# Attention stage of a transformer block: products with v in one piece a unit, images with doubled rows, norms and x + half on other engines, later x loads

## What is computed

```
x = x + 0.5 * ffn(layernorm(x))       # stage pair 1
x = x + rwkv6(layernorm(x))           # recurrence
x = x + 0.5 * ffn(layernorm(x))       # stage pair 2, same weights

def ffn(z):
    h = layernorm(z) * ln1_w + ln1_b
    q, k, v = h @ w_qkv                       # 16 heads of 8 channels
    z = z + softmax(q k^T / sqrt(8)) v @ w_proj
    h = layernorm(z) * ln2_w + ln2_b
    e = argmax(h @ gate_w + gate_b)           # one of 8 experts a token
    return z + gelu(h @ w1[e]) @ w2[e]
```

## Time and profile before

| | |
|---|---|
| median of 3 runs | 1475.89 us (1472.48 to 1477.49) |
| profiled execution | 1473.18 us, its span 1471.4 us |
| TensorE busy | 1230.9 us, 84% of the span |
| VectorE busy | 1042.9 us, 71% |
| ScalarE busy | 860.7 us, 58% |
| POOL busy | 553.6 us, 38% |
| granted TensorE clock, mean | 0.909 |
| moved by DMA | 82.40 MB, 56 GB/s |

### The profile page before, as it was taken

The page is one execution under the profiler, slowest core; times in us unless marked ns, Lnnn a source line. Parts: engine busy times, 40 slices in busy tenths (PEclk is TensorE's granted clock), DMA queues, the critical chain, the costliest instruction groups (busy, mean ns, idle before and its releaser), DMA issues. The chain is left out here.

```text
span 1471.4 us, 36051 instructions
## 1 busy us (share of the span) xinstructions
PE 1230.9 (84%) x12512; PEld 661.3 (45%) x12513; DVE 1042.9 (71%) x1842; ACT 860.7 (58%) x1742; POOL 553.6 (38%) x797
## 2 busy tenths in 40 slices
PE   2799999999997596398888754999999999993893
PEld 1234444444443596145455442344444444442893
DVE  3889988988992332478788745888898988963232
ACT  2288877778775353444334411588788778881451
POOL 6122324323212354355676536222332431222462
PEclk9599999999999799599999955799999999996896
DMA  4322442222110121100000003122122122100224
GB/s 117 71 74 74 130 121 68 82 71 73 55 36 9 53 67 47 42 2 3 3 2 2 3 1 87 57 75 65 49 82 73 53 81 66 56 15 30 56 66 122
DMA packets 81540, 82.40 MB, mean 56 GB/s; under 512 B 16249, under 2 KB 53724, under 8 KB 81392
## 3 DMA queue, kind: packets, MB, share of 16 engines
q1 hardware_dynamic: 72560, 69.88, 16.7%
q0 software_dynamic: 4608, 8.44, 1.8%
q10 hardware_dynamic: 4224, 2.10, 0.5%
HBM read 50.42 MB, written 29.93 MB: 55 GB/s over the span
## 5 line engine op out<-in xcount | busy, mean ns | idle before, releaser
L986 DVE TENSOR_REDUCE maxima<-ps 128x2 f32<-128x1024 f32 x512 | 616.2, 1222 | 89.8 <-PE ps L652 88.5
L933 ACT ACTIVATE probs<-ps 128x512 f32<-128x512 f32 x1024 | 550.8, 600 | 120.3 <-PE ps L660 109.7
L652 PE MATMUL ps<-k_stack,q_stack 62*128 62x512 f32 x1024 | 390.0, 473 | 39.0 <-DVE maxima L986 21.7
L660 PE MATMUL ps<-q_stack,k_stack 64*128 64x512 f32 x1024 | 396.3, 464 | 4.2 <-ACT q_whole L869 3.4
L670 PE MATMUL ps<-probs,v_stack 128*32 128x256 f32 x4096 | 329.6, 394 | 0.9 <-ACT probs L933 0.4
L652 PEld LDWEIGHTS ps<-k_stack,q_stack 62*128 62x128 f32 x1024 | 160.1, 194 | 235.9 <-issue 138.3
L660 PEld LDWEIGHTS ps<-q_stack,k_stack 64*128 64x128 f32 x1024 | 159.2, 187 | 30.5 <-ACT q_whole L869 8.6
L670 PEld LDWEIGHTS ps<-probs,v_stack 128*32 128x32 f32 x4096 | 81.7, 108 | 166.6 <-issue 148.3
L532 POOL CAST neg_wide<-maxima 128x16 fp32r<-128x16 f32 x64 | 12.6, 196 | 286.7 <-DVE maxima L986 286.7
L1299 POOL DMA_INDIRECT expert_out<-yt,number x80 | 78.3, 979 | 72.4 <-POOL number L1295 44.1
L1276 DVE COPY w_now<-w 128x512 f32 x80 | 34.6, 433 | 80.1 <-issue 42.2
(11 more groups left out here) (208 smaller groups left out, 1622.7 us busy)
## 6 DMA issues: line engine op xcount, KB each, us to landing
q_stack<-q_split SPq DMA_DIRECT2D x256, 64.0 KB
k_stack<-k_split SPq DMA_DIRECT2D x512, 32.0 KB
q_split<-q_parts SPq DMA_DIRECT2D x16, 512.0 KB, 2.7
k_split<-k_parts SPq DMA_DIRECT2D x16, 512.0 KB, 3.6
xt<-sorted SPq DMA_DIRECT2D x80, 64.5 KB
w<-in_L_ffn_w SPq DMA_DIRECT2D x16, 256.0 KB, 3.0
rows<-expert_out SPq DMA_DIRECT2D x16, 256.0 KB, 4.5
x_all<-in_L_attn_x SPq DMA_DIRECT2D x8, 256.0 KB, 5.1
```

Source lines behind the costliest of these rows:

```text
L652: mm = t.matmul(psS[:, h, :], qs[g][score_rows(h), h // 2, u * P:(u + 1) * P], ks[g][score_rows(h), h // 2, :], start=True, stop=True)
L660: t.matmul(ring("e", G, u, n), ks[G % NG][half(h), h // 2, u * P:(u + 1) * P], qs[G % NG][half(h), h // 2, :], start=True, stop=True).then ...
L933: a.activation(probs[u % 2][:, h, :], ring("e", G, u, n), ACT.Exp, scale=float(DK) ** -0.5).then_inc(e_read, 1)
L986: v.tensor_reduce(maxima[G % 2][:, :, pair, u:u + 1], psS[:, 2 * pair:2 * pair + 2, :], AX_X, ALU.max, negate=True).then_inc(s_read, 1)
```

## The change

In one unit, all four score and exponent pairs now come first, and the products with v of the unit before follow in one call of 512 queries a head. `q_split` and `k_split` in DRAM have 32 rows a head for 16: SP stores each part twice, in the order of the stack, and a group is loaded with 4 transfers. The second norm and the norm of the rows go to ScalarE, as Identity with a scale and a bias; the bias is minus the mean times the scale, which VectorE and POOL prepare (`less`, `shift`, `p_less`, `p_shift`). The first norm on POOL is two operations on 512 columns. x + half goes to POOL, as two operations. `choose` puts the statistics of a later batch between its steps, `places` the inversion. turn_h goes from (3,0) to (3,2) and v from (3,2) to (3,0). Six of the eight x slices and the routing constants are loaded after the first barrier. At a stage's start two low parts go ahead of four memsets on VectorE; at its end half of the paddings go to ScalarE's queue.

```diff
             for dst, src in first:
                 sp.dma_start(dst[:], src).then_inc(loaded, 16)
-            for j in range(SL):
+            for j in range(2):
...
-            for dst, src in routing:
-                sp.dma_start(dst[:], src).then_inc(s["routing_loaded"], 16)
...
-        PER_LOAD = 16 * 12
+        PER_LOAD, STORED = 16 * 4, 16 * SPLITS
...
+                def store_q(j):
+                    sp.wait_ge(low["q"], j + 1)
+                    for a in range(SPLITS):
+                        half_rows = qd[a * SPLITS * DK:(a + 1) * SPLITS * DK, :, j * SW:(j + 1) * SW]
+                        sp.dma_start(half_rows.rearrange("(c i) h t -> (i h) c t", i=DK),
+                                     parts["q"][:].bitcast(F32)).then_inc(stored["q"], 16)
...
                     for e in range(2):
-                        for a in range(SPLITS):
-                            row = HALF * e + a * SPLITS * DK
-                            sp.dma_start(qs[g][row:row + SPLITS * DK, :, :].bitcast(F32),
-                                         heads_of(qd, 0, SPLITS * DK, e)).then_inc(loaded[g], 16)
-                            for at in (row, row + DK):
-                                sp.dma_start(ks[g][at:at + DK, :, :].bitcast(F32),
-                                             heads_of(kd, a * DK, DK, e)).then_inc(loaded[g], 16)
+                        here = slice(HALF * e, HALF * e + ROWS)
+                        sp.dma_start(qs[g][here, :, :].bitcast(F32), heads_of(qd, e)).then_inc(loaded[g], 16)
+                        sp.dma_start(ks[g][here, :, :].bitcast(F32), heads_of(kd, e)).then_inc(loaded[g], 16)
...
+                def halve(p):
+                    x, half_of = x_all[:, tiles_in(p), :], half_one[:].unsqueeze(2).broadcast_to([P, ST, P])
+                    pool.wait_ge(x1_ready, p + 1)
...
+                    g_.tensor_tensor(half_x1[:], x1[:], half_of, ALU.mult).then_inc(half_made, 1)
+                    pool.wait_ge(half_made, p + 2)
+                    g_.tensor_tensor(x, x, half_x1[:], ALU.add).then_inc(halved, 1)
...
-                def pv(unit, part):
+                def pv(unit):
...
-                    here = slice(part * T // 2, (part + 1) * T // 2)
                     for h in range(GROUP):
-                        last = t.matmul(psO[VW * h:VW * (h + 1), here], vs[g][:, u, h, :], probs[u % 2][:, h, here],
+                        last = t.matmul(psO[VW * h:VW * (h + 1), :], vs[g][:, u, h, :], probs[u % 2][:, h, :],
...
-                        if ahead:
-                            score(G + 2, u, 0)
-                        exponent(G, u, 0)
-                        if ahead:
-                            score(G + 2, u, 1)
-                        exponent(G, u, 1)
-                        if u != 1:
-                            values(0)
-                        if ahead:
-                            score(G + 2, u, 2)
-                        exponent(G, u, 2)
+                        for n in range(GROUP):
+                            if ahead:
+                                score(G + 2, u, n)
+                            exponent(G, u, n)
                         if u == 1:
-                            values(0)
-                        if ahead:
-                            score(G + 2, u, 3)
-                        exponent(G, u, 3)
-                        values(1)
+                            pe.wait_ge(v_staged, G + 1)
+                            if g % SHARE == 0 and G:
+                                pe.wait_ge(o_kept, shared(b, g))
+                        if unit:
+                            pv(unit - 1)
...
+                def norm_second(j, tiles):
+                    act.wait_ge(shift_made, j + 1)
+                    act.wait_ge(turned, j)
+                    for q in tiles:
+                        last = a.activation(zn[:, q, :], x_all[:, j * ST + q, :], ACT.Identity, bias=shift[j % 2][:, q:q + 1],
+                                            scale=scales[j % 2][:, 1, q:q + 1])
...
+                        if b + 2 < B and (g, u) in ((1, 0), (1, 1)):
+                            norm_second(b + 2, range(2 * u, 2 * u + 2))
+                        if 1 <= b < B - 1 and (g, u) in ((3, 0), (3, 1)):
+                            norm_rows(b - 1, range(2 * u, 2 * u + 2))
+                        if b == B - 1 and (g, u) == (2, 3):
+                            norm_rows(b - 1, range(ST))
...
+                for k in "qk":
+                    low_part(0, k)
                 for i in range(2):
                     for e in range(2):
                         v.memset(ks[i][HALF * e + ROWS:HALF * e + STACK, :, :].bitcast(F32), 1.0).then_inc(k_set, 1)
-                for j in range(2):
-                    for k in "qk":
-                        low_part(j, k)
+                for k in "qk":
+                    low_part(1, k)
```

More of the change, by code:

```diff
@@ L239, in load_constants, with load_early @@
     x_slices = slices_of(d["L0_attn_x"])
+    def load_early(sp):
+        for j in range(2, SL):
+            here = slice(j * ST, (j + 1) * ST)
+            sp.dma_start(x_all[:, here, :], x_slices[:, here, :]).then_inc(s["x_loaded"][j], 16)
+        for dst, src in routing:
+            sp.dma_start(dst[:], src).then_inc(s["routing_loaded"], 16)
     def load_late(sp, part):
@@ new lines, in store_q, with store_k @@
+                def store_q(j):
[4 more added lines that the diff above has]
+                                     parts["q"][:].bitcast(F32)).then_inc(stored["q"], 16)
+                def store_k(j):
+                    sp.wait_ge(low["k"], j + 1)
+                    for a in range(SPLITS):
+                        every_other = kd.rearrange("(c a i) h t -> a c i h t", c=SPLITS, a=SPLITS)[a, :, :, :, j * SW:(j + 1) * SW]
+                        sp.dma_start(every_other.rearrange("c i h t -> (i h) c t"),
+                                     parts["k"][:].bitcast(F32)).then_inc(stored["k"], 16)
@@ L469, in place @@
                                      max_rows[G % 2][e * count:(e + 1) * count, :].bitcast(F32)).then_inc(rows_placed, 16)
-                store(0, "q", qd)
-                store(0, "k", kd)
+                if load is not None:
+                    load[0](sp)
+                store_q(0)
+                store_k(0)
                 for g in range(NG):
                     load_group(0, g)
-                store(1, "q", qd)
-                store(1, "k", kd)
+                store_q(1)
+                store_k(1)
                 place(0)
@@ L603, in _ @@
                         low_part(b + 2, "q")
+                    if g == 3 and b >= 1:
+                        halve(b - 1)
                     if G + 2 <= LAST:
@@ L853, in copy_o, with norm_rows @@
                                  ACT.Copy).then_inc(o_copied, 1)
+                def norm_second(j, tiles):
[4 more added lines that the diff above has]
+                                            scale=scales[j % 2][:, 1, q:q + 1])
+                    if tiles[-1] == ST - 1:
+                        last.then_inc(normed, 1)
+                def norm_rows(p, tiles):
+                    act.wait_ge(p_shift_made, p + 1)
+                    act.wait_ge(y_turned, p + 1)
+                    for q in tiles:
+                        last = a.activation(rows[:, p * ST + q, 0:P], x1[:, q, :], ACT.Identity, bias=p_shift[:, q:q + 1],
+                                            scale=rstd[:, q:q + 1])
+                    if tiles[-1] == ST - 1:
+                        last.then_inc(row_ready, 1)
                 def keep_z(j):
@@ L936, in _ @@
                 for kind, j in AFTER:
+                    if kind == "turn_h":
+                        norm_rows(j, range(ST))
                     job(kind, j)
+                act.wait_ge(pads_ready, 1)
+                for e in range(E // 2, E):
+                    row = act.value_load(pad_row[0:1, e:e + 1], min_val=0, max_val=E * (TOK + P) - P)
+                    act.dma_start(xs[ds(row, P), :], s["padding"][:, 0, :]).then_inc(act_padded, 16)
+                act.wait_ge(act_padded, 16 * (E - E // 2))
             @block.vector
@@ L970, in norm_both @@
                         vec.wait_ge(turned, j)
-                    for q in tiles:
+                    for q in range(ST):
                         last = v.tensor_scalar(zn[:, q, :], x_all[:, j * ST + q, :], moments[j % 2][:, q, 0:1],
                                                scales[j % 2][:, 1, q:q + 1], ALU.subtract, ALU.mult)
-                    if tiles[-1] == ST - 1:
-                        last.then_inc(normed, 1)
+                    last.then_inc(normed, 1)
                 def low_part(j, k):
@@ L1041, in row_moments, with choose @@
                     if p:
-                        vec.wait_ge(rstd_ready, p)
+                        vec.wait_ge(p_shift_made, p)
+                    v.tensor_scalar(p_less[:], p_moments[:, :, 0], -1.0, None, ALU.mult)
```

(10 more changed lines are left out.)

139 lines of the change are left out of this document (66 added, 73 removed).

## The result

The changed kernel takes **1512.9 us** (median of 4, 1508.7 to 1515.4), the kernel before 1474.7 beside it: ratio 1.0255, 95% interval 1.0221 to 1.0289. It is slower, and the forecast of 1509 lies among its runs; its terms fare less well than its sum, as the table shows. The profiled execution is 1513.6 in span, against 1471.4. Medians are over fast runs; the only profile taken of a slow one is experiment 2's, 1509.7 us where its fastest run took 1485.3.

The account below looks back on a forecast made before the run. Attention stages dominate; after the change, ScalarE's reading of the three-bank exponent ring holds TensorE. Stages +52, starts -10.3 and -2.9, ends -6 sum to +33 on 1473.2: 1506, or 1509 against the median; range 1484 to 1532.

Parts of the forecast that it names:

- The unit: Four heads, 128 keys in attention: the fourth exponent waits for ScalarE to read the first's bank; 2.63 us, 0.15 more.
- Rival 1: Attention units: the ring doesn't hold and fewer changes of array use win; 1399 us, chance 0.11.
- rival 2: Attention units: the held exponent's weights are already in place, so a unit is 2.45 us; 1466 us, chance 0.08.
- The delays: Full attention batch: ScalarE's jobs and added norms put off first exponents, 4.2 us together, 2.2 of it the norms.
- what delays the first exponent now counts in full: Attention units: delays up to about 0.37 us, free before, now cost; ScalarE's jobs delay by 0.23 to 1.0.
- those on VectorE go: Full attention batch: of today's 3.2 us of waits for VectorE or ScalarE, VectorE's vanish and 0.3 stay.
- nobody waits for VectorE: Expected sign in the attention profile after the change: no engine waits for VectorE, with some 42 of 56 us busy.
- Batch 7: Last attention batch: eight units without scores add 3.0 us, four norms in one place 1.1; +3.8 with small gains.
- Rival 3: TensorE's clock falls, slower still: a tenth of the units cold add 38 us; 1547 us, chance 0.04.
- The end of a stage: Paddings on two queues end with the scatters, -3.9 us; norms and shift give back 0.9: -3.0, twice -6.
- The start: Before first scores: earlier barrier -7.3 us, images and memsets -2.9 in each stage; -10.3 and -2.9 in all.
- the 1.3 and the earlier q eat most of that up: Stage start: doubled stores' extra 2.5 us mostly hidden by k's low part starting 1.3 earlier and by earlier q.

Follow-up runs that it names:

- experiment 2: Changed kernel with products still in one piece, but issued between a unit's third and fourth exponents, all four scores ahead of the third: 1498.6 us (1485 to 1507).
- experiment 1: Changed kernel with the products with v back in two halves at their old places: 1467.3 us, ratio 0.9953 to the kernel before.
- experiment 8: Changed kernel, products in one piece, with a ring of two PSUM banks instead of three: 1683.3 us (one run).
- experiment 11: Kernel before with one part of the change alone, products with v in one piece: 1501.7 us, ratio 1.0185.
- experiment 4: Changed kernel with both norms (second of the input, that of the rows) back on VectorE, products in one piece: 1491.2 us.
- experiment 12: Changed kernel with only batch 7's four norms of the rows back on VectorE, products in one piece: 1504.7 us.
- experiment 3: Changed kernel with all eight padding transfers back on SyncE's queue, none on ScalarE's: 1506.0 us.
- experiment 10: Changed kernel with products in two halves, both norms on VectorE, and the earlier q and k images (rows once, twelve loads a group): 1458.5 us.

## Why the prediction was right, step by step

**The unit: right.** "0.55 + 0.60 + 0.05 = 1.20. Then come 0.43 to the products and 1.00 for them" is the row of the profile after, to 0.01; experiments 1, 2 and 8 show the same sum from three other sides. Rival 1 (the fewer changes win) is out by experiment 11, rival 2 (weights of the held exponent in place) by the row itself: that weight load waits 0.42 and starts no earlier than its matmul. The Trainium skill (TensorE: Matmul & The Clock Gate, "Step-by-step: what each phase is for") has the queue pull weight loads ahead of matmuls in flight; in this wait the trace does not show it (weights at 283.72, their matmul at 283.73).

**The delays: the sum near, its terms too large.** For a full batch the forecast had +2.4 for the hold, +2.0 for the delays by ScalarE's jobs, +2.2 for the norms and -2.9 for waits that go when VectorE has less to do: +3.7. The runs show +2.1 for the one piece alone (experiment 11; 3.1 from experiment 1 to the changed kernel), where hold and jobs had 4.4; -0.7 for the rest of the change without the norms (experiments 11 to 4); and +1.6 for the norms, in which VectorE's relief by them is counted already: together +2.9. So "what delays the first exponent now counts in full" is mis-sized, by 1.3 to 2.3, and so is "those on VectorE go", the other way. The sign "nobody waits for VectorE" did not come. The scores' weights wait for the maxima for 87.7 us in 158 waits, and in the kernel before, by the same view, for 88.6 in 158:

```profile
PEld ps L652 <- DVE maxima L986: 88.6, 158, 1.6
```

That these errors met is luck; why the one piece costs no more stays open. Batch 6 was forecast at +1.0 and shows nothing, and up to batch 2's logits 3.4 and 1.9 us less were lost than forecast; I did not look for the cause of these.

**Batch 7: the size wrong, by the clock.** Forecast were +3.0 for the units, +1.1 for "four norms in one place" and -0.3 of small gains. Without a fall of the clock the batch is +2.6: 1.7 for the units (42.06 in experiment 12 for 40.34) and 0.8 for the norms. What failed is that nothing stood in the sum for the clock, which adds 2.3 us in one stage and 5.5 in the other. Rival 3 had the mechanism, but I looked for it in the busy share of whole stages. The forecast's chance for it, 0.04 for a fall over a tenth of the units, left out one short idle in a place where TensorE had slack already.

**The end of a stage: the sign wrong.** "On two queues they end with the scatters: -3.9" is the failed step. They do end with the scatters, but the experts' load does not follow: from the counted experts to it are 14.5 and 14.1 us, 13.2 before, and 13.0 and 12.8 in experiment 3. The last traffic of the first stage ends by 502, the load comes at 508.31; what fills that stretch the rows don't show, and I did not try it apart. The paddings were never what the phase waited for. From the last group's gate to the counts another 3.5 and 3.1 us were lost. The norms explain none of it: with them on VectorE (experiment 4) it takes 25.1 and 23.5 us, for 24.0 and 24.4 in the changed kernel and 20.4 and 21.4 before. What goes with it is again the clock. In the 28 stages of the fourteen profiles this stretch takes 20.4 to 22.9 us where the clock is at 0.50 for at most 16.1 us of it, and 23.3 to 25.8 where it is for 16.8 or more; in the kernel before it stays at 1.00 for the first 12.8 of 20.4 us and the first 7.8 of 21.4. That the clock is the cause is argued: no experiment changed it alone.

**The start: right, and half of it wrong.** The barrier gives what was forecast (statistics at 5.71). From the statistics to the scores the first stage gained 1.9 us (24.18 to 22.33) and the second 0.6, where images and memsets were to give 2.9 in each. Experiment 10 puts what the images give at 0.6 in the second stage, and has them lose 0.2 in the first: "the 1.3 and the earlier q eat most of that up" undersold the stores.

So the unit was foreseen, but that the sum came within 4 us of the median is partly luck, because errors met: the first, the full and the sixth batches were overrated by 14 us together (eight full ones by 0.8), batch 7 and the ends underrated by 20, the starts by 3.

## What to carry to other kernels

Before removing a split in a stream of matmuls, list which waits its second half covers: with three banks in a ring, four users in a row pay for one reading by the other engine, wherever the row is cut. Moving work off an engine with slack onto the engine that empties the ring is priced by what still covers that ring (here 0.7 or 1.6 us a batch). And when a lump of work goes into a stretch where TensorE has slack, add to its length (here 0.8 us) what TensorE's clock may do behind it (here up to 5.5).

## What the runs showed of the hardware that I had not expected

One idle of 1.31 us in a stretch in which TensorE was busy 3.0 of 4 us was followed by a granted clock of 0.50, and the same products took 1.94 us instead of 1.06; an idle of 1.32 us in the same place in another execution (experiment 3) was not. With idles of 0.45 us a unit in the same place (experiment 12) it stayed at 1.00 beyond the end of batch 7. And from the first of the doubled stores to the first load it took 7.0 us at the start of the first stage in every kernel that has them, and 7.0 to 9.1 at the start of the second; the cause was not sought.
